# A fused attention and mixture-of-experts block on one core: PE takes over the sum over experts, POOL and ACT take small steps from DVE, and the set-up is split

## The reference

```
x = x + conv(ln_c(x));  t = tokens(x);  t = t + ffn(ln_t(t))
conv: q, k, v = W_qkv x + b;  4 heads of 32
      q = softmax(q, over the 32 of a head) / sqrt(32);  k = softmax(k, over the 4096 tokens);  v = v / 4096
      context = k v^T;  out = W_out (context^T q) + b_out;  layer norm over the channels, times g_ln
ffn:  p = softmax(t router_w + router_b) over 8 experts;  the 2 largest, scaled to sum to 1
      sum over those 2 of p_e * (t expert_w[e] + expert_b[e])
```

## Time and profile before

| | |
|---|---|
| runs | 448.45 us median of 3 (447.31 to 449.0) |
| the profiled execution's own time | 451.15 us |
| its span, first to last instruction | 449.4 us |
| PE busy | 334.0 us (74%) |
| DVE busy | 335.0 us (75%) |
| ACT busy | 224.3 us (50%) |
| POOL busy | 201.9 us (45%) |
| granted TensorE clock, mean | 0.918 |

### The profile page before, as it was taken

The page is one execution under the profiler, slowest core; times in us unless marked ns, Lnnn a source line. Parts: engine busy times, 40 slices in busy tenths (PEclk is TensorE's granted clock), DMA queues, the critical chain, the costliest instruction groups (busy, mean ns, idle before and its releaser), DMA issues.

```text
span 449.4 us, 7711 instructions
## 1 busy us (share of the span) xinstructions
PE 334.0 (74%) x2896; PEld 198.6 (44%) x2896; DVE 335.0 (75%) x467; ACT 224.3 (50%) x385; POOL 201.9 (45%) x189
## 2 busy tenths in 40 slices
PE   0044175988888999799889988988997997765470
PEld 0034062453455555456445645554554545334250
DVE  7844347736659999999999999899899748534860
ACT  1020224658827955685578377736745872540000
POOL 8110100014405825762666276537733862773470
PEclk9999659899969999999999999999999998985585
DMA  2210203003211330332033113301230120012001
GB/s 63 89 51 0 64 7 71 1 2 85 79 26 32 87 72 3 71 107 58 1 92 120 27 25 80 84 1 45 74 74 1 33 67 21 15 37 66 15 32 47
DMA packets 13516, 21.66 MB, mean 48 GB/s; under 512 B 5254, under 2 KB 5288, under 8 KB 13480
## 3 DMA queue, kind: packets, MB, share of 16 engines
q1 hardware_dynamic: 13480, 21.17, 17.9%
HBM read 4.38 MB, written 4.19 MB: 19 GB/s over the span
## 4 chain that ended last, share of the span: by engine, by line
PE 47%; DVE 22%; SPq 8%; issue 7%; ACT 5%; DMA 4%; POOL 4%; POOLq 0%; PEldq 0%; DVEq 0%
PE narrow L896 22%; PE wide L896 14%; SPq L351 8%; PE small L896 6%; PE sums L899 4%; DVE stack L647 2%; DMA out_dram<-y_out 2%; DMA stack<-high 2%; DVE kmax L768 2%; DVE gated L851 2%; DVE nqmax L749 2%; DVE stack L649 2%; POOL xhat L481 1%; POOL low L486 1%; PE wide L899 1%
## 5 line engine op out<-in xcount | busy, mean ns | idle before, releaser
L466 POOL TENSOR_TENSOR paired<-gated 128x512 f32<-128x512 f32 x64 | 81.3, 1282 | 69.7 <-PE sums L899 59.6
L851 DVE TENSOR_TENSOR gated<-wide,gates 128x1024 f32<-128x1024 f32 x64 | 75.6, 1217 | 16.2 <-PE wide L896 11.0
L896 PE MATMUL wide<-w_stack,stack 128*128 128x256 f16 (+1 forms) x512 | 61.2, 262 | 14.7 <-DMA stack<-high 6.8
L447 POOL TENSOR_TENSOR xhat<-centered,rstd 128x992 f32<-128x992 f32 x8 | 15.0, 1872 | 124.8 <-PE small L896 90.4
L896 PEld LDWEIGHTS wide<-w_stack,stack 128*128 128x128 f16 x512 | 41.2, 104 | 47.3 <-issue 27.0
L545 ACT ACTIVATE ek<-narrow,wscale 128x512 f32<-128x512 f32 x64 | 40.6, 685 | 21.7 <-PE small L896 11.6
L749 DVE TENSOR_REDUCE nqmax<-wide 128x32 f32<-128x1024 f32 x32 | 38.9, 1219 | 15.4 <-PE wide L896 15.3
L899 PE MATMUL sums<-ident,paired 128*128 128x128 f32 x256 | 42.2, 297 | 10.4 <-POOL paired L466 6.8
L764 DVE TENSOR_TENSOR eq<-eq,wide 128x1024 f32<-128x1024 f32 x32 | 39.0, 1218 | 13.2 <-PE wide L896 13.2
L556 ACT ACTIVATE eq<-narrow,wscale 128x512 f32<-128x512 f32 x64 | 41.1, 681 | 9.7 <-PE narrow L896 9.0
L899 PEld LDWEIGHTS sums<-ident,paired 128*128 128x128 f32 x256 | 31.0, 151 | 25.8 <-POOL paired L466 12.3
(11 more groups left out here) (147 smaller groups left out, 601.7 us busy)
## 6 DMA issues: line engine op xcount, KB each, us to landing
stack<-high SPq DMA_DIRECT2D x128, 64.0 KB, 2.0
x_in<-in_x_dram SPq DMA_DIRECT2D x8, 512.0 KB
stack<-low SPq DMA_DIRECT2D x64, 64.0 KB, 2.0
out_dram<-y_out SPq DMA_DIRECT2D x8, 512.0 KB
w_rows<-in_L_ffn_expert_w_dram SPq DMA_DIRECT2D x3, 32.0 KB
g_col<-in_L_conv_g_ln_dram SPq DMA_DIRECT2D x4, 0.1 KB
w_nat<-in_L_conv_w_qkv_dram SPq DMA_DIRECT2D x1, 48.0 KB
w_rows<-in_L_ffn_router_w_dram SPq DMA_DIRECT2D x3, 1.0 KB
```

The lines of the kernel that those rows point to most:

```text
L447: nc.gpsimd.tensor_tensor(xhat[:, b % 2, :, 1:C], centered1[:].rearrange("p (g c) -> p g c", c=C)[:, :, 1:C], rstd1[:].unsqueeze(2).broadc ...
L466: nc.gpsimd.tensor_tensor(paired[:, n % PAIREDS, :, :, :], gated[:, n % GATEDS, 0:E // 2, :, :], gated[:, n % GATEDS, E // 2:E, :, :], ALU ...
L851: nc.vector.tensor_tensor(gated[:, n % GATEDS, :, :, :].rearrange("p e t c -> p t e c"), src.rearrange("p (t e c) -> p t e c", t=4, e=E), ...
L896: return nc.tensor.matmul(dst, lhs, rhs, start=start, stop=stop)
```

## The change

PE sums over the experts alone: `add_experts` transposes all eight gated experts instead of four sums, `pairs` on POOL and the buffer `paired` are gone, `gated` has four buffers instead of three, and PE waits for DVE's `gate` directly. The ones rows are no longer written by five DVE instructions into the stacks: DVE writes one row block `ones16`, and SP copies it by five transfers (256 KB each) into the stacks; PE waits for all five at the end of the set-up. `set_up` is cut in two on DVE (`set_up_operands`, `set_up_scales`) and on PE (`set_up_transposes`, `set_up_maxima`), with places of their own in the order, and uses `sums` instead of `wide`; the first part waits only for three weights. `bout_rep` and `g_col` are loaded from ACT's queue. The splitting of the maxima moves from DVE to POOL (`query_max_parts`, `key_max_parts`). The probabilities move from four DVE steps to ACT (`probabilities`) and one to POOL (`g2`). Some buffers are contiguous instead of every second element. The order table is new on every engine, with PERIOD 2443 instead of 2817.

```diff
-EKS, GATEDS, PAIREDS, XINS, X2S, STACKS = 4, 3, 2, 4, 3, 3
+EKS, GATEDS, XINS, X2S, STACKS = 4, 4, 4, 3, 3
-PERIOD, STEPS = 2817, range(86931)
+PERIOD, STEPS = 2443, range(58227)
-SETUP = {'pe': 22774, 'dve': 36226, 'act': 36195}
+SETUP = {'transposes': 18731, 'maxima': 20170, 'operands': 28696, 'scales': 29047, 'act': 28120}
...
+            def fill_ones(stack):
+                sp.dma_start(stack[96:P, :].rearrange("c (j i) -> c j i", j=J),
+                             ones16[96:P, :].unsqueeze(1).broadcast_to([P - 96, J, N // J])).then_inc(ones_copied, 16)
...
-            for b in range(1, XINS):
+            load(1)
+            sp.wait_ge(ones_made, 1)
+            fill_ones(stack1[:, 0, :])
+            for b in range(2, XINS):
                 load(b)
+            for k in range(1, STACKS):
+                fill_ones(stack1[:, k, :])
+            for k in range(2):
+                fill_ones(stack3[:, k, :])
...
+            def query_max_parts(b, half):
+                c = query_steps
+                pool.wait_ge(wide_free, wide_turn["qmax", b, 2 * half + 1] + 1)
+                if b > 0:
+                    pool.wait_ge(narrow_full, narrow_turn["qrows", b - 1, half] + 1)
+                c.inc(nc.gpsimd.tensor_copy(qmax_nat[:, half, 0, :], nqmax[:, half, :]))
+                c.wait()
+                nc.gpsimd.tensor_tensor(qmax_nat[:, half, 1, :], nqmax[:, half, :], qmax_nat[:, half, 0, :],
+                                        ALU.subtract).then_inc(qmax_nat_ready, 1)
+            def key_max_parts(b):
+                c = key_steps
+                pool.wait_ge(nkmax_ready, b + 1)
+                if b > 0:
+                    pool.wait_ge(small_full, small_turn["krow", b - 1, 0] + 1)
+                c.inc(nc.gpsimd.tensor_copy(kmax_nat[:, 98:99], nkmax[:]))
+                c.wait()
+                nc.gpsimd.tensor_tensor(kmax_nat[:, 99:100], nkmax[:], kmax_nat[:, 98:99],
+                                        ALU.subtract).then_inc(kmax_nat_ready, 1)
...
                 pool.wait_ge(probs_ready, b + 1)
+                pool.wait_ge(picked, b + 1)
+                c.inc(nc.gpsimd.tensor_tensor(g2[:], g1[:], e2[:], ALU.mult))
...
-            def pair_experts(b, u):
-                nc.gpsimd.tensor_tensor(paired[:, n % PAIREDS, :, :, :], gated[:, n % GATEDS, 0:E // 2, :, :],
-                                        gated[:, n % GATEDS, E // 2:E, :, :], ALU.add).then_inc(paired_ready, 1)
...
-            def second_exp(b):
+            def probabilities(b):
+                c = prob_steps
                 act.wait_ge(gap_ready, b + 1)
+                c.inc(nc.scalar.activation(e2[:], gap[:], ACT.Exp, scale=wscale[:, 2:3]))
+                c.wait()
+                c.inc(nc.scalar.activation(den[:], e2[:], ACT.Ln, bias=1.0))
+                c.wait()
+                c.inc(nc.scalar.activation(den[:], den[:], ACT.Exp, scale=-1.0))
+                c.wait()
+                nc.scalar.activation(g1[:], den[:], ACT.Copy, scale=wscale[:, 1:2]).then_inc(probs_ready, 1)
...
             def constants():
-                for k in range(STACKS):
-                    nc.vector.memset(stack1[96:P, k, :], 1.0).then_inc(stacks_made, 1)
-                for k in range(2):
-                    nc.vector.memset(stack3[96:P, k, :], 1.0).then_inc(stacks_made, 1)
+                nc.vector.memset(ones16[96:P, :], 1.0).then_inc(ones_made, 1)
...
-                pe.wait_ge(paired_ready, n + 1)
+                pe.wait_ge(wide_free, wide_turn["experts", b, v] + 1)
-                for e in range(E // 2):
-                    ins = tr(dst, paired[:, n % PAIREDS, e, :, :].rearrange("p t c -> p (t c)"), ident[:],
-                             start=(e == 0), stop=(e == E // 2 - 1))
-                ins.then_inc(paired_used, 1)
+                for e in range(E):
+                    ins = tr(dst, gated[:, n % GATEDS, e, :, :].rearrange("p t c -> p (t c)"), ident[:],
+                             start=(e == 0), stop=(e == E - 1))
+                ins.then_inc(gated_used, 1)
```

More of the change, by code:

```diff
@@ new lines @@
+    "qexp": (21350, 21350, 21435, 21626, 22491, 22494, 22540, 22540),
+    "xt": (18555, 18730),
+    "z": (21771, 22712),
+    "qrows": (21235, 21889),
+    "attend": (23534, 23535),
+    "var2": (23582, 23582),
+    "cent3": (23898, 24009),
+    "var3": (24046, 24061),
+    "kexp": (21734, 22187, 22190, 22695, 22721, 22722, 22913, 23158),
+    "bc": (22494, 22509, 22911, 22911),
+    "experts": (26424, 26502, 26548, 26620, 26733, 26735, 27147, 27581),
+    "kmax": (20763, 21084, 21084, 21139),
@@ new lines @@
+    "qmax": (21099, 21111, 21186, 21382),
+    "xc": (20169,),
+    "router": (25159,),
+    "krow": (21648,),
+    "sums": (22791, 22820, 22838, 23144, 23159, 23159, 23160, 23160),
+    "mix": (23348,),
+    "out": (26562, 26688, 26829, 27318, 27432, 28215, 28660, 28687),
+    "root1_act": (26538,),
+    "high3": (31271, 31391),
+    "high1": (27302,),
+    "e2": (33152,),
+    "logit_act": (32212,),
+    "qexp_act": (28120, 28132, 28365, 28662, 29296, 29298, 29557, 29557),
+    "xt_act": (25215, 25378),
@@ new lines @@
+    "kmax_dve": (29428, 29749, 29752, 30175),
+    "kred": (30630,),
+    "qmax_dve": (29779, 29783, 30734, 30879),
+    "low1": (29046,),
+    "route": (34065, 34065, 34145, 34159, 34805, 34805, 35432, 35432, 35433, 35567, 35625, 35687),
+    "qparts": (35725, 37163),
+    "kparts": (36898,),
+    "gates": (41125,),
+    "low3": (40051, 40259),
+    "xhat3": (39649, 39860),
+    "x2": (38678, 38678),
+    "scale1": (35380,),
+    "fill3": (15882,),
+    "fill1": (12198,),
+    "store": (20223,),
@@ L705, in set_up @@
                 dve.wait_ge(setup_t, 3)
-                st.inc(nc.vector.tensor_copy(wscale[:], wide[:, 0, 0:3]))
+                st.inc(nc.vector.tensor_copy(wscale[:], sums[:, 256:259]))
                 st.wait()
```

253 lines of the change are left out of this document (103 added, 150 removed).

## The result

The changed kernel takes 439.25 us (median of 4 runs, 432.99 to 443.27) against 448.73 for the kernel before in the same sitting (4 runs, 447.31 to 449.18): ratio 0.9695, 95% interval 0.9616 to 0.9775. So it is faster, by 9.5 us at the medians where I predicted 40, and lies outside my range of 393 to 428. The ratio leaves out two runs of the changed kernel that lie over 1.5% above its fastest; by it the gain is 13.7 us. The profiled execution is the fastest run, 432.99 us with a span of 431.1.

What follows compares the result with a forecast made beforehand. DVE was taken to set the full periods before, PE after; 35 + 26.5 + 40 + 40 + 4 x 40.6 + 38.5 + 67 = 409.4 against 449.4, 40 less, so 448.45 - 40 = 408 us, range 393 to 428.

Steps and rivals of the forecast that it cites:

- So PE becomes the bound: Full periods: PE's 38.7 us of issue plus 1.9 for coupling, 40.6 instead of 42.05, 5.6 over four; bounds 38.7 and 42.5.
- my 3.5: PE in full periods: 32 more transposes per batch cost 3.5 us by their starts, four costing 0.43.
- The rival of the clock: Full stretches: clock falls to a mean of 0.9, PE with coupling needs 45 a period, 430 us in all; chance 0.07.
- `gap` too may gain 1: DVE in full periods: `gap` waits for POOL, which loses eight additions, so it may get 1 us shorter.
- no `gap` or `tie` of over 1 us: Sign expected in the profile: none of these DVE steps over 1 us beside a long POOL instruction.
- The start: Up to the next `xt`: 35 instead of 62.0, 27 us less, bounds 18 and 31; batch 0's keys at 33.
- copies and loads hold the start: Rival: ones' copies and loads hold the start up to 44, coupling eats the periods' gain (42); 423 us, chance 0.16.
- First period: Batch 0's first period, set by its own chain: 26.5 us, 6 less than 32.7; bounds 25 and 33.
- the end: Last stretches, POOL's additions and probabilities off the way: 2 us less of 69, so 67.
- The third stretch: Third period after the start: 38.8 us before, 40 with the transposes, 1 more.
- POOL's queue: Rival, slower than before: key maximum parts wait behind `gates`; 8w for a wait w per period, 456 at w = 6; chance 0.05.
- DVE's idle time ahead of the first `gated`: Sign in the loop: DVE idle about 1 us once a batch, since `gate` waits for POOL's gate steps.

Runs made afterwards that it cites:

- with the loads early: Changed kernel with SP issuing each later load of x (batches 4 to 7) right behind the previous fill1: 427.55 us, 0.9526 of the kernel before.
- without the multiplication: Changed kernel, loads of x issued early, POOL's multiplication by rstd2 left out: 414.43 us; with a constant written in its place: 415.14 us.
- with the constant: Changed kernel, loads of x issued early, POOL writing a constant to an unread buffer in place of the multiplication by rstd2: 415.14 us, 0.9284 of the kernel before.
- with the multiplications moved: Changed kernel, loads of x issued early, POOL's two multiplications by rstd2 put behind the sums x2, into an unread buffer: 427.44 us, 0.9518 of the kernel before.
- With the fill ahead: Changed kernel with batch 0's fill1 ahead of x of batches 2 and 3 and the other four copies of ones: 430.74 us, 0.9503 of the kernel before.
- the two versions that moved a maximum: On the 416.12 us version (both SP orders, POOL's late wait for the pick), third query maximum ahead of the ties: 415.12 us; ahead of `gap`: 412.59 us.
- the start alone: Kernel before with only the changed start (ones by copies, loads, set-up in parts), its loop untouched: 432.05 us, 0.9611 of the kernel before.

## Why the prediction was wrong

**The step that failed** is the last term of "So PE becomes the bound ... I add 1.9: **40.6 instead of 42.05**": 1.9 us for all waits of PE in a full period. The four periods are 44.0 in the mean, beyond my bound of 42.5, 5.3 us above PE's 38.7.

PE's own part held. Eight transposes start within 0.88 us:

```profile
201.83 1.04 PE L925 MATMUL sums<-ident,gated 128*128 128x128 f32 x8
202.71 0.38 PE L922 MATMUL narrow<-stack,w_stack 128*128 128x512 f16 x1
```

Four took 0.43, so 32 more cost 3.6 us against my 3.5. (The 38.98 us busy isn't the same thing as my 38.7 of issue: before, PE was busy for 38.0 at 35.2 of issue.) The rival of the clock didn't come: it is 1.00 in the periods with short waits.

Of the 5.3 us, an estimate from the periods of three versions (44.0 as changed, 42.4 with the loads early, 40.4 to 40.5 without the multiplication) puts 1.6 on SP's order, 2 on the stalls, and leaves 1.7.

- The stalls. I wrote "`gap` too may gain 1", and "no `gap` or `tie` of over 1 us" as a sign, because POOL loses eight additions. They come from whatever POOL reads at that moment; the additions went, and `scaled` and x2 moved under DVE's route steps (201.25 to 206.8 above). 2.1 us a period, shown by the runs with the constant and with the multiplications moved. I had also read the trace of before wrongly. There `gap` stood beside POOL's `xhat`, which the change keeps, and not beside an addition:

```profile
173.21 1.28 DVE L826 TENSOR_TENSOR gap<-top 128x32 f32<-128x32 f32 x1
172.58 1.86 POOL L447 TENSOR_TENSOR xhat<-centered,rstd 128x992 f32<-128x992 f32 x1 [7.63 <-PE small L896]
```

- No term of the sum held SP's order within the loop: the table now has a load of x ahead of `fill1` where a batch waits for it. It cost up to 3.7 us in a period (46.2 in place of the 42.5 without), 1.4 of it as longer products at the lower clock behind the wait (PE busy 40.39 instead of 38.98), and 7.6 us over the whole.

That the versions without the multiplication come to 40.4 and 40.5, my 40.6, is in part luck. With "PE becomes the bound", 3.5 us less of PE would have to take the same off such a period, and it took 1.3.

**The start** was the right mechanism and a wrong size: 22 us saved, not 27. First keys at 39.4 instead of 33. I took a value between "nothing beyond the loads" and the loads' rate for the copies; the last copy landed at 38.6, later than the 36 that the loads' rate gives. With the fill ahead the keys come at 31.6, where the set-up ends (my 30.1), so the queue held 7.8 us. The set-up itself is 1.3 us late because its second part stands behind `low1`, which ends 2.3 us later than I had it.

The rival "copies and loads hold the start" came nearer than the forecast: its start of 44 is 3.8 us from the measured 40.2, mine of 35 is 5.2, and the measured periods of 44.0 are nearer to its 42 than to my 40.6.

**The rest held.** First period 27.8 for 26.5, 39.3 for 40, the stretch after the full ones 39.4 for 38.5, the end 66.0 for 67. The third stretch, 42.5 for 40, is a full period already and failed with them. POOL's queue made no wait of PE for `kmax_nat` in each period. DVE's idle time ahead of the first `gated` was 0.86 us, as said (about 1).

**What stays open**: what sets 40.5 together with PE once the stalls are gone, and how all three steps could be kept off POOL's reads in the whole computation; the two versions that moved a maximum freed one each.

## What to carry to other kernels

When work leaves an engine, ask of each stall that is to vanish which instruction will stand beside it then, and move steps that a neighbour can't stall (here maxima from PSUM) into that place. List SP's queue in order like any other engine's: a large transfer that nobody waits for soon, issued just ahead of small ones that somebody waits for at once, can hold one of these for several us (landings of 5.9 and 6.5 us instead of 2.0 here); and moving the small one ahead only pays if the displaced one isn't next. Part a gain by running the start alone and the loop alone: here the start brought the whole of it, and the loop gained only once the wait for its transfers and a stall were taken out.

## What the runs showed of the hardware

I had not expected SP to be held in issuing. At the start, SP's issues of the copies of ones (256 KB each, timeline of the changed kernel), beside a usual issue later:

```profile
13.00 10.04 SPq L343 DMA_DIRECT2D stack<-ones  x4
24.24 0.56 SPq L353 DMA_DIRECT2D stack<-high  x1
```

Four issues took 10.04 us, the longest 6.27, where the others take 0.6: `fill1`'s could not have been issued at 22 even had `low1` been ready. With the fill ahead and the copies behind it, the same four took 0.68, 0.66, 0.66 and 1.43 us.

The transfers that PE waited for were held long past their own 2 us, but not all that stood behind the large ones were. These are two parts of the first stack, the one issued at 26.17 (2.53 us to landing) and the one at 26.81 (2.75), as the profile rounds them:

```profile
stack<-high SPq DMA_DIRECT2D x1, 64.0 KB, 2.5
stack<-low SPq DMA_DIRECT2D x1, 64.0 KB, 2.8
```

They were issued behind the one of 25.48 and landed some ten us ahead of it. In each quarter only the third part, the one into rows 64 to 95, was late (13.76, 12.37, 10.86 and 9.51 us), and behind the load of x in the loop it was the third part too (5.94 us, issued at 228.26; its neighbours 2.6 each). The Trainium skill (DMA: Bandwidth & Descriptors, "Queues, rings and completion order") says that a transfer's count on its semaphore lands only after every earlier write of the same transfer engine. That would fit the late parts if they share engines with the copies and loads; no run here shows which engines a transfer used, so why it is the third part stays open.

The stalls of DVE beside POOL's reads aren't confined to steps with two inputs. In the earlier trace rows `qmax_nat` and `den`, a cast and a step with one tensor, were among the long ones, and in the set-up of the changed kernel a copy that took 0.18 us before takes 1.88 while POOL makes `xhat` (17.82 to 19.82); there it cost nothing, since DVE soon waits 2.5 us for `high1`:

```profile
17.98 1.88 DVE L710 COPY headcols<-headmask 128x32 f32<-128x32 f32 x1
```
